# Stores of layer two issued about 25 stages behind their last join, in a macaron block of two routed expert layers around an attention layer

## The chip, the cores and the metric

The kernel runs on one core of a Trainium2 chip. The metric is the device time of one execution in microseconds (us). Three runs of the kernel before took 816.01, 818.97 and 826.0 us; their median is 818.97 us.

## The reference, cut to what matters

The input x has 8 x 512 tokens of 256 values (float32). Three residual layers follow each other, the first and the last with the same weights:

```python
x = x + 0.5 * ffn(layernorm(x), gate_w, w1, w2, w3)     # layer one of experts
x = x + attn(layernorm(x), W_q, W_k, gain, bias, ...)    # top-8 causal neighbours, softmax, gelu
x = x + 0.5 * ffn(layernorm(x), gate_w, w1, w2, w3)     # layer two of experts

def ffn(x, gate_w, w1, w2, w3):                         # 8 experts, 2 of them per token
    probs = softmax(x @ gate_w.T)
    weights, idx = top_k(probs, 2);  weights /= sum(weights)
    out_all = (silu(x @ w1[e].T) * (x @ w3[e].T)) @ w2[e].T      # for each expert e
    return sum over the 2 chosen experts of weights * out_all
```

The change touches only the last step: writing the finished x to the output after layer two.

## The kernel before, in words

The 4096 tokens are 32 token tiles of 128 tokens, and x stays in SBUF (`t_X`) for the whole kernel. An expert layer works like this. The router picks two experts for each token, and GpSimd scatters the split (high and low float16) normalised rows into a list per expert in HBM (`hs`). These lists are cut into 71 expert tiles of 128 rows for each layer, so 142 in all; numbers 0 to 70 belong to layer one, 71 to 141 to layer two. For one expert tile n the work is a pipeline over five engines:

- SyncE (SP in the profile) issues `load` (L1059), a DMA transpose from `hs` to `t_ht`. The ring has four buffers.
- TensorE does `up` (L1227), two groups of 6 matmuls into PSUM; ScalarE does `tanh` (a SiLU, L1360), VectorE `gate` (L1726), ScalarE `high` (L1369) and VectorE `glow` (L1732). The last two write the high and low halves of the gated activation to one of four buffers: three are called `t_gp`, the fourth lies in `t_W`.
- SyncE issues `gt` (L1097), a DMA transpose of these halves to `t_gh` (or, for each fourth tile, within `t_W`). It waits for `glow` of its tile. `high` of tile n waits until the `gt` of tile n-4 has landed, because it overwrites the buffer that was read.
- TensorE does `down` (L1239), 12 matmuls, after the `gt` has landed. ScalarE copies the result out of PSUM (`evict`, L1376), and GpSimd issues `put` (L1000), an indirect DMA that scatters the rows to `yt` in HBM at their token positions.

When all expert tiles that can hold rows of a token tile have been put, SyncE issues `fetch` (L1112): a load of two token tiles (512 KB; the last two are of one tile, 256 KB) from `yt` into `t_hp` or `t_s`. VectorE then does `join` (L1741), two instructions per token tile that add the weighted rows to `t_X`. At the end SyncE issues the ten stores named `out` (L1131 to L1135): seven of four token tiles (512 KB), one of two tiles and two of one tile. Each waits for the joins of its tiles on VectorE and then issues one DMA on SyncE's queue. After the last, SyncE waits for all ten (L1136) and the kernel ends. A transfer by SyncE never waits for VectorE once it is issued; an instruction on SyncE holds up everything behind it on SyncE while it waits or issues.

Nothing on the chip sets the order. Each operation is one letter of a string, `ORDER` (L126 to L155), which is a list of stages: `g` is `out`, `U` is `join`, `J` is `fetch`, `Q` is `gt`, `*` is `put`, `W` is `load`. `Plan.run` (L185 to L205) reads it from left to right. At each letter it takes the waiting operation of this kind with the smallest key, or, with a digit behind the letter, the one at that place of the sorted list. A letter fixes the place of an operation in the sequence of its own engine and no more: a letter of SyncE that is moved leaves the sequences of the other engines as they were. Below, store 0 is the store of token tiles 0 to 3, store 4 that of tiles 4 to 7, and so on.

Of the kernel before, what the change touches and what calls it, by code (L numbers as in the profile page):

```python
# [93 lines left out]
class Want:  # L94
# [55 lines left out]
    "~WWW*s1[hSShPP~~!!*^.N>;V;>^QhQ;WFFu.N;|~h>.EE;!|SS!||**~FF;*~NP.P_~~EQ>;_*F*E~;>~~~EF.*WWQSNNFWQ_S_~;QP.;P>;.S;"  # L150
    ">*N~~S~NPP;.;EEFFWQSPN>;.;EN*uW*uF*W~~E>QSF*~_~;.;NW>;EQQQPSPFS;E>E;.FFWPy1N***SPWEQu;.N>;;S>FQy~WQ.NS_W~Q~*~PP;"
    "E.EQQ;>;;NWWuF_FsSP.N_*>SEP~;;*EFEF*.NSWPyQQQWE>;FF**.;>;~~~.*WNSEEF*~~~P;WuQ>N;S.;NSFPPQQEF**~~>;.;>NSPW;.W;WEE"
    "FNSPQQFEF>;;>***.;.;NNSSWPPJJU>;.;>NUU;SE.;>;;NSWQFPUJJUP>;.NS.UUUWQWJ;>NEFuWPE;JUUUUJJU.FE;>;;>WQNS.UUUN~~~QJFS"
    ";SW;>E**PP.NFJUUUUQJu;;EQWE.SFPP>;;WQJQWE**FF.UNSNP>;;.NSQ*>P*U;*.S;>NSPEEFF**U;U;Q.NSg1gPgPQQ*EEF*FEF*QQE*FJJU*"
    "EEUUFFU*J*g2JgJg1gUUUUggg")  # L155


class Plan:
# [1697 lines left out]
```

## Time and profile before

| | |
|---|---|
| median of three runs | 818.97 us (816.01 to 826.0) |
| the profiled execution's own time | 820.86 us |
| its span, from the first to the last instruction | 819.3 us |
| outside the span | 1.56 us |
| busy: PE, DVE, ACT, POOL | 85%, 69%, 61%, 56% |
| HBM read, written | 33.96 MB, 44.81 MB |
| queue of SyncE (q1): share of the 16 DMA engines' time | 66.8% |
| stores `out`: first and last issue | 788.8 and 816.3 us |

PE is TensorE's matmuls, PEld its weight loads, DVE VectorE, ACT ScalarE, POOL GpSimd, SPq the sequencer of SyncE. The share of the DMA engines is the time that packets are under way on them; in short stretches it passes 1, since packets of one engine overlap. The joins run from 751.1 to 816.2 us, beside the last 14 expert tiles; all that the change moves lies in the last 60 us.

### The profile page before, as it was taken

Reading aid. Unit: us, or ns where it says so; the run is one execution under the profiler, and the core shown is the slowest. Engines: PE = TensorE matmul, PEld = TensorE weight load, DVE = VectorE, ACT = ScalarE, POOL = GpSimd, SP = SyncE. Lnnn points to the kernel's source line nnn. Section 1 sums busy time; section 2 is a strip of 40 time slices with the busy share of each in tenths; the row PEclk is TensorE's granted clock in tenths of the full one; section 3 lists DMA queues with packets and bytes.
Section 4 is the critical chain, followed back from the end, with each engine's and each line's share of the span. In section 5 each row is a group of like instructions: output and inputs, shape, how many; then the busy total and the mean of one; then the engine's idle time right before and its main releaser. Section 6 shows DMA issues by size and latency. Waiting matters only on the chain.

```text
span 819.3 us, 17367 instructions
## 1 busy us (share of the span) xinstructions
PE 694.5 (85%) x4608; PEld 425.3 (52%) x4608; DVE 562.8 (69%) x1596; ACT 498.8 (61%) x972; POOL 456.4 (56%) x545
## 2 busy tenths in 40 slices
PE   1741557999989999999998999999999899999982
PEld 1631224565446665565665555656555456655552
DVE  6779871434577888789889888997766533335953
ACT  4657633444359986877889698976866334343330
POOL 3458888537242645657477654775757854453132
PEclk9965789999999999999999999999999999999997
DMA  8957468888885977889988797899787887779999
GB/s 331 427 198 163 127 175 214 153 158 155 182 155 111 173 150 142 193 162 207 172 172 179 158 197 140 171 180 159 152 164 157 186 173 149 133 146 206 285 247 295
DMA packets 321973, 151.52 MB, mean 185 GB/s; under 512 B 302493, under 2 KB 305949, under 8 KB 321117
## 3 DMA queue, kind: packets, MB, share of 16 engines
q1 hardware_dynamic: 303997, 112.77, 66.8%
q0 software_dynamic: 17888, 37.65, 16.4%
q8 instruction: 46, 0.75, 0.4%
q14 instruction: 42, 0.34, 0.1%
HBM read 33.96 MB, written 44.81 MB: 96 GB/s over the span
## 4 chain that ended last, share of the span: by engine, by line
PE 42%; SPq 13%; DMA 12%; DVE 12%; issue 8%; POOL 6%; ACT 5%; another core or an unknown queue 1%; POOLq 0%; DVEq 0%; ACTq 0%
PE B L1227 22%; PE B L1239 13%; POOL hs L953 4%; SPq L1097 4%; SPq L1059 3%; DMA t_gh<-t_gp 3%; SPq L1044 2%; DMA t_ph<-t_s 2%; PE B L1252 2%; DMA t_ph<-t_p 2%; DMA yt<-t_W,t_idx 1%; PE B L1266 1%; DVE t_th L1726 1%; PE B L1163 1%; DVE t_gp L1732 1%
## 5 line engine op out<-in xcount | busy, mean ns | idle before, releaser
L1227 PE MATMUL B<-t_W,t_ht 128*128 x1704 | 400.2, 383 | 19.6 <-issue 11.3
L1227 PEld LDWEIGHTS B<-t_W,t_ht 128*128 128x128 f16 x1704 | 166.3, 98 | 198.6 <-issue 35.8
L1000 POOL DMA_INDIRECT yt<-t_W,t_idx x107 | 112.2, 1048 | 131.5 <-ACT t_W L1376 97.3
L1726 DVE SCALAR_TENSOR_TENSOR t_th<-B,t_K,t_th 128x512 f32<-128x512 f32 x142 | 105.6, 746 | 108.1 <-PE B L1227 78.6
L1239 PE MATMUL B<-t_W,t_gh 128*128 x1284 | 159.5, 275 | 11.3 <-DMA t_gh<-t_gp 5.7
L953 POOL DMA_INDIRECT hs<-t_s,t_POS x112 | 116.1, 1037 | 65.2 <-issue 28.6
L1239 PEld LDWEIGHTS B<-t_W,t_gh 128*128 128x128 f16 x1284 | 124.4, 99 | 46.7 <-issue 17.3
L1360 ACT ACTIVATE t_th<-B,t_K 128x512 f32<-128x512 f32 x142 | 96.4, 681 | 52.1 <-PE B L1227 34.6
L1732 DVE TENSOR_TENSOR t_gp<-t_th,t_gp 128x512 f16<-128x512 f32 x107 | 75.8, 714 | 34.8 <-ACT t_gp L1369 26.2
L1369 ACT ACTIVATE t_gp<-t_th 128x512 f16<-128x512 f32 x107 | 66.1, 623 | 55.1 <-DVE t_th L1726 36.7
L992 POOL DMA_DIRECT2D t_idx<-hs x142 | 80.3, 570 | 29.3 <-DMA yt<-t_W,t_idx 14.8
L1376 ACT ACTIVATE t_W<-B 128x256 f32<-128x256 f32 x107 | 40.1, 375 | 81.5 <-PE B L1239 50.9
L1000 POOL DMA_INDIRECT yt<-t_yo,t_idx x35 | 36.9, 1054 | 38.5 <-ACT t_yo L1376 28.7
L1324 ACT ACTIVATE t_hp<-t_X,t_ve 128x256 f32<-128x256 f32 x96 | 49.5, 589 | 12.5 <-DVE t_ve L1574 10.5
L942 POOL TENSOR_TENSOR t_ve<-t_ve,t_mhalf 128x4 f32<-128x4 f32 x24 | 27.0, 1125 | 53.6 <-DVE t_ve L1568 52.7
L1239 PE MATMUL B<-t_W 128*128 x420 | 51.8, 273 | 4.4 <-DMA t_W<-t_W 2.6
L1239 PEld LDWEIGHTS B<-t_W 128*128 128x128 f16 x420 | 40.2, 98 | 14.4 <-issue 5.9
L1009 POOL TENSOR_TENSOR t_hp<-t_hp,t_W 128x256 f32<-128x256 f32 x32 | 27.5, 860 | 25.3 <-DVE t_hp L1804 24.9
L1741 DVE SCALAR_TENSOR_TENSOR t_X<-t_hp,t_CW,t_X 128x256 f32<-128x256 f32 x64 | 32.0, 511 | 13.4 <-DMA t_hp<-yt 12.3
L1305 ACT ACTIVATE t_W<-t_W,t_SC 128x1024 f16<-128x1024 f32 x24 | 26.9, 1141 | 19.4 <-DVE t_W L1528 9.1
L1585 DVE TENSOR_TENSOR t_s<-t_hp,t_s 128x256 f16<-128x256 f32 x88 | 36.3, 460 | 1.9 <-ACT t_s L1334 1.9
L1360 ACT ACT_TABLE_LOAD x28 | 35.9, 1283 | 0.5
(206 smaller groups left out, 902.3 us busy)
## 6 DMA issues: line engine op xcount, KB each, us to landing
t_W<-wk SPq DMA_DIRECT2D x6, 2048.0 KB, 15.8
t_hp<-yt SPq DMA_DIRECT2D x16, 512.0 KB
t_s<-yt SPq DMA_DIRECT2D x15, 512.0 KB
t_X<-x SPq DMA_DIRECT2D x8, 512.0 KB, 7.8
out<-t_X SPq DMA_DIRECT2D x7, 512.0 KB
hs<-t_ph SPq DMA_DIRECT2D x22, 136.0 KB
t_ht<-hs SPq DMA_TRANSPOSE x142
t_idx<-hs POOLq DMA_DIRECT2D x142, 0.5 KB
```

The source lines that it names most:

```text
L953: eng.indirect_dma_start(hs_d[L], bass.IndirectOffsetOnAxis(ap=POS[:, k, t + j:t + j + 1], axis=0), SROW[slot][:, 2 * h + j, :], None).the ...
L992: eng.dma_start(IDX[:, n % RING:n % RING + 1].bitcast(F16), hs_d[L][bass.ds(place[n], 128), 512:514]).then_inc(d_id[n % RING], 16)
L1000: eng.indirect_dma_start(yt_d[L], bass.IndirectOffsetOnAxis(ap=IDX[:, n % RING:n % RING + 1], axis=0), YO[n % YR], None).then_inc(d_y[n % ...
L1227: t = eng.matmul(B[b][:], HT[n % HTR][:, (2 * hl + db) * 128:(2 * hl + db) * 128 + 128], W16[:, bass.ds(expert[n] * 4096 + (db * 2048 + wl ...
L1239: t = eng.matmul(B[b][:, 0:256], GH[n % LAG][:, gl, fb * 128:fb * 128 + 128], W16[:, bass.ds(expert[n] * 2048 + (W2OFF + wl * 1024 + fb * ...
L1324: eng.activation(hp[:, j, :], X[:, t0 + j, :], ACT.Identity, bias=ve[:, 2, j:j + 1], scale=ve[:, 1, j:j + 1]).then_inc(s_hp, 1)
L1360: eng.activation(TH[n % THR][:], B[b][:], ACT.Silu, scale=K[:, 0:1]).then_inc(free[b], 1)
L1369: eng.activation(GP[n % LAG][:, 0, :], TH[n % THR][:], ACT.Copy).then_inc(s_gh, 1)
L1376: eng.activation(YO[n % YR], B[b][:, 0:256], ACT.Copy).then_inc(free[b], 1)
L1585: eng.tensor_tensor(s16[:, j, 256:512], hp[:, j, :], s16[:, j, 0:256], ALU.subtract).then_inc(s_lo, 1)
L1726: eng.scalar_tensor_tensor(out=th[:], in0=B[b1][:], scalar=K[:, 7:8], in1=th[:], op0=ALU.mult, op1=ALU.mult).then_inc(free[b1], 1)
L1732: eng.tensor_tensor(gp[:, 1, :], th[:], gp[:, 0, :], ALU.subtract).then_inc(s_gl, 1)
```

## The change

The diff is in `ORDER` only: seven `g` leave their places and stand elsewhere.

```diff
-    "FNSPQQFEF>;;>***.;.;NNSSWPPJJU>;.;>NUU;SE.;>;;NSWQFPUJJUP>;.NS.UUUWQWJ;>NEFuWPE;JUUUUJJU.FE;>;;>WQNS.UUUN~~~QJFS"
-    ";SW;>E**PP.NFJUUUUQJu;;EQWE.SFPP>;;WQJQWE**FF.UNSNP>;;.NSQ*>P*U;*.S;>NSPEEFF**U;U;Q.NSg1gPgPQQ*EEF*FEF*QQE*FJJU*"
-    "EEUUFFU*J*g2JgJg1gUUUUggg")
+    "FNSPQQFEF>;;>***.;.;NNSSWPPJJU>;.;>NUU;SE.;>;;NSWQFPUJJUP>;.NS.UUUWQWJ;>NEFuWPgE;JUUUUJJU.FEg;>;;>WQNS.UUUN~~~QJ"
+    "gFS;SW;>E**PP.NFJUUUgUQJu;;EQWE.SFPP>;;WQJQWE**gFF.UNSNP>;;.NSQ*>P*U;*.S;>NSPEEFF**U;U;Q.NSPPQQ*EEF*FEF*QQE*gFJJ"
+    "U*EEUUFFU*J*JJgUUUUggg")
```

The sequences of TensorE, VectorE, ScalarE and GpSimd stay as they are; only SyncE's is another. Two places matter. The first is the stretch of SyncE's sequence around the fetches of token tiles 10 to 21. `t_ht<-hs` is a `load`, `t_gh<-t_gp` and `t_W<-t_W` are a `gt`, `t_s<-yt` and `t_hp<-yt` are a `fetch`, and `out<-t_X` a store. Before:

```order
L1112 DMA t_s<-yt 128x1024
L1112 DMA t_hp<-yt 128x1024
L1112 DMA t_s<-yt 128x1024
L1059 ISA
L1059 DMA_TRANSPOSE t_ht<-hs 128x4x128
L1097 DMA_TRANSPOSE t_gh<-t_gp 128x8x128
L1097 DMA_TRANSPOSE t_W<-t_W 128x8x128
L1112 DMA t_hp<-yt 128x1024
L1059 ISA
L1059 DMA_TRANSPOSE t_ht<-hs 128x4x128
L1112 DMA t_s<-yt 128x1024
L1097 DMA_TRANSPOSE t_gh<-t_gp 128x8x128
```

And now:

```order
L1135 DMA out<-t_X 128x1024
L1112 DMA t_s<-yt 128x1024
L1112 DMA t_hp<-yt 128x1024
L1112 DMA t_s<-yt 128x1024
L1135 DMA out<-t_X 128x1024
L1059 ISA
L1059 DMA_TRANSPOSE t_ht<-hs 128x4x128
L1097 DMA_TRANSPOSE t_gh<-t_gp 128x8x128
L1097 DMA_TRANSPOSE t_W<-t_W 128x8x128
L1112 DMA t_hp<-yt 128x1024
L1135 DMA out<-t_X 128x1024
```

Stores 0, 4 and 8 are shown in their new places; store 12 follows right behind the second `t_s<-yt`, ahead of the `gt` of expert tile 132. Store 0 now stands ahead of the fetch of tiles 10 and 11, store 4 ahead of the `load` of expert tile 137 and of the `gt` of 130, store 8 ahead of the `load` of 138.

The second place is the end of SyncE's sequence, from the `gt` of expert tiles 136 and 137 on. Before:

```order
L1097 DMA_TRANSPOSE t_gh<-t_gp 128x8x128 x2
L1135 DMA out<-t_X 128x1024 x3
L1097 DMA_TRANSPOSE t_gh<-t_gp 128x8x128
L1097 DMA_TRANSPOSE t_W<-t_W 128x8x128
L1097 DMA_TRANSPOSE t_gh<-t_gp 128x8x128 x2
L1112 DMA t_hp<-yt 128x1024
L1112 DMA t_s<-yt 128x1024
L1112 DMA t_hp<-yt 128x1024
L1135 DMA out<-t_X 128x1024
L1112 DMA t_s<-yt 128x512
L1135 DMA out<-t_X 128x1024
L1112 DMA t_s<-yt 128x512
```

And now:

```order
L1135 DMA out<-t_X 128x1024
L1097 DMA_TRANSPOSE t_gh<-t_gp 128x8x128 x3
L1097 DMA_TRANSPOSE t_W<-t_W 128x8x128
L1097 DMA_TRANSPOSE t_gh<-t_gp 128x8x128 x2
L1135 DMA out<-t_X 128x1024
L1112 DMA t_hp<-yt 128x1024
L1112 DMA t_s<-yt 128x1024
L1112 DMA t_hp<-yt 128x1024
L1112 DMA t_s<-yt 128x512 x2
L1135 DMA out<-t_X 128x1024
```

The three stores (4, 0, 8) between the `gt` of 137 and the `gt` of 138 are gone; store 16 stands ahead of the `gt` of 136, and store 20 ahead of the fetches of tiles 24 and on. Ahead of the last two fetches there were stores 20 and 12, and behind them 24 and 16; now only store 24 is left there, behind both fetches. The last three stores (256, 128 and 128 KB) close the sequence in both.

## Rows read from the trace of the kernel before

**Rows 1.** The page: busy time and share by engine; DMA share in 40 slices.

```profile
PE 694.5 (85%) x4608; PEld 425.3 (52%) x4608; DVE 562.8 (69%) x1596; ACT 498.8 (61%) x972; POOL 456.4 (56%) x545
...
DMA  8957468888885977889988797899787887779999
```

**Rows 2.** Chain that ended last, from 740 us: start us, us, what.

```profile
761.74 5.86 DMA t_hp<-yt
...
769.57 2.76 PE B L1227 x12
...
783.45 0.85 issue
...
791.04 7.54 DMA t_gh<-t_gp
...
798.73 4.30 PE B L1239 x36
...
803.08 2.84 another core or an unknown queue
...
807.09 4.28 DMA yt<-t_W,t_idx
...
811.43 3.79 DMA t_s<-yt
...
815.76 0.48 DVE t_X L1741
```

**Rows 3.** Stretches: busy us of PE, PEld, DVE, ACT, POOL; clock, DMA share, GB/s.

```profile
20.00:30.00 10.00, 4.89 (x59) 4.29 (x60) 7.23 (x36) 7.08 (x14) 1.01 (x1) 1.00 1.01 431
770.00:780.00 10.00, 9.99 (x64) 6.08 (x63) 9.33 (x19) 4.08 (x8) 1.88 (x2) 1.00 1.16 270
814.00:816.00 2.00, 0.00 (x0) 0.00 (x0) 1.02 (x3) 0.00 (x0) 0.00 (x0) 0.50 1.05 422
```

**Rows 4.** SyncE's instructions in order of time: start us, us, what.

```profile
761.18 0.52 SPq L1112 DMA_DIRECT2D t_s<-yt  x1
...
764.26 2.61 SPq L1097 DMA_TRANSPOSE t_gh<-t_gp  x1
...
772.31 1.23 SPq L1097 DMA_TRANSPOSE t_gh<-t_gp  x1
...
788.82 2.02 SPq L1135 DMA_DIRECT2D out<-t_X  x3
791.04 3.67 SPq L1097 DMA_TRANSPOSE t_gh<-t_gp  x1
...
810.82 0.43 SPq L1135 DMA_DIRECT2D out<-t_X  x1
...
811.93 4.81 SPq L1135 DMA_DIRECT2D out<-t_X  x5
```

**Rows 5.** ScalarE's instructions in order of time, with the idle before and its releaser.

```profile
771.70 0.63 ACT L1369 ACTIVATE t_gp<-t_th 128x512 f16<-128x512 f32 x1 [4.25 <-DMA t_gh<-t_gp]
...
777.45 0.63 ACT L1369 ACTIVATE t_gp<-t_th 128x512 f16<-128x512 f32 x1 [1.78 <-DMA t_gh<-t_gp]
```

**Rows 6.** VectorE's joins of token tiles 14 and 15, in order of time.

```profile
770.15 1.92 DVE L1741 SCALAR_TENSOR_TENSOR t_X<-t_s,t_CW,t_X 128x256 f32<-128x256 f32 x4
```

**Rows 7.** The ten stores: issue time on SyncE, ns min/median/max, first and last.

```profile
L1135 SPq DMA_DIRECT2D out<-t_X x10: 433/543/1243, 788.8 to 816.3; - x10
```

**Rows 8.** TensorE's instructions in order of time, with the idle before.

```profile
798.73 1.50 PE L1239 MATMUL B<-t_W,t_gh 128*128 x12 [1.25 <-DMA t_gh<-t_gp]
```

**Rows 9.** SyncE's waits in the last 20 us: us in total, times, longest.

```profile
SPq L1137 <- DMA out<-t_X: 2.3, 1, 2.3
```

**Rows 10.** Columns as in Rows 3; a thinly filled stretch of TensorE and its clock.

```profile
648.00:652.00 4.00, 2.38 (x10) 0.77 (x8) 1.12 (x2) 0.99 (x3) 3.39 (x5) 1.00 0.59 183
...
656.00:660.00 4.00, 2.58 (x9) 1.14 (x10) 1.50 (x2) 1.85 (x4) 3.38 (x5) 0.82 1.03 237
```

**Rows 11.** TensorE: one tile's `up` at the lower clock, in order of time.

```profile
657.42 4.22 PE L1227 MATMUL B<-t_W,t_ht 128*128 x12 [2.27 <-DVE t_th L1726]
```

## The prediction, made before the changed kernel ran

> **What bounds the kernel now.** I read the page first. TensorE is busy for 85% of the span and the DMA engines for most of it, with nines in the last four slices, which is where the stores are [rows 1]. Then I followed the chain that ended last from 740 us on, to see which wait ends last at each point [rows 2]. It goes through a fetch of 5.86 us at 761.74 (token tiles 12 and 13, on which a join waits that stands ahead of a gate), then almost without a break through TensorE to 789 us, through a `gt` transpose of 7.54 us from 791.04 to 798.59, through the last `down` groups on TensorE, a piece of 2.84 us that the profile gives to no queue that it knows (the 36 matmuls before it end at 803.03 and the last 12 follow with 1.4 us, so 1.5 us of it lie behind TensorE's end), the last `put` with 4.28 us, the last fetch with 3.79 us, the last join and the last store. Third, stretches and SyncE's timeline: TensorE is busy for 9.99 of 10 us in 770 to 780 while the DMA engines stand at a share of 1.16 [rows 3]. So in this part two resources are nearly full at the same time, TensorE and the DMA engines, and behind 804 us there is only a chain of transfers.
>
> **What the change removes, adds and moves.** The amount of work is the same: ten stores, the same bytes. Only SyncE's sequence is another. Seven stores of 512 KB move; six of them go to an earlier place in the sequence, and the seventh (24) stays near its place but comes behind the last two fetches. Prices of one such store: on SyncE 0.54 us of issue in the median, 1.24 at most [rows 7]; on the DMA engines its bytes at the best rate that the trace shows over 10 us, 431 GB/s at a share of 1.01 [rows 3]: 524 KB / 431 GB/s = 1.22 us, my estimate.
>
> The Trainium skill ("DMA: Bandwidth & Descriptors", section Specifications) gives about 358 GB/s as the limit of HBM for one core. By it a store would be 1.46 us and the sum below -0.5 instead of -0.75. The trace speaks against that limit here, with 431 GB/s over 10 us of loads.
>
> Step A, **stores 0, 4, 8 and 12 go in between 761 and 773 us.** Do they wait for joins? The last join that one of them needs is that of tile 15; it ends at 770.15 + 1.92 = 772.07 [rows 6], and store 12 stands right ahead of the `gt` that was issued at 772.31 [rows 4]. So waiting costs nothing; what is queued behind them pays for issue and transfer. Store 0 stands ahead of the fetch at 761.18, and so of the one at 761.74 that the chain passes. Stores 0 and 4 stand ahead of the `gt` at 764.26 [rows 4] (expert tile 130), which landed just before 771.70: ScalarE stood idle for 4.25 us until then [rows 5]. It has no slack. All four stand ahead of the `gt` at 772.31 (tile 132), for which ScalarE waited 1.78 us until 777.45 [rows 4, 5]. Both `gt` are read by TensorE right away. Lower end of the price: 0, if the stores fill gaps between the transposes (270 GB/s in 770 to 780 against 431 at best [rows 3]). Less than nothing is excluded, since everything in this stretch stands behind the added stores. Upper end: four transfers of 1.22 and four issues of 0.54, all in a row: 4.9 + 2.2 = 7.1 us. I take **+2.4 us**, two transfers: those that stand ahead of the `gt` with no slack. What comes later is partly covered, as TensorE then has its own queue of `up` groups; the DMA share of 1.16 says that it won't be near zero.
>
> Step B, **stores 4, 0 and 8 leave the place at 788.82.** There they took SyncE 2.02 us. The `gt` behind them (tile 138) was issued at 791.04 and took SyncE 3.67 us [rows 4], landed 7.54 us after its issue [rows 2], and TensorE stood idle for 1.25 us until it had landed [rows 8]. With the stores gone it is issued about 2 us earlier and no longer stands behind 1.5 MB (3.7 us). TensorE is full before it and the other three `gt` are in time, so only the idle time comes back: **-1.25 us**; ends 0 (something else is late then, the `gt` of 139 to 141) and -1.25. Store 16 goes in two `gt` ahead of 788.82, before the `gt` of 136. TensorE reads that after 24 more matmuls of `down` and 12 of `up`, over 5 us of its own work (36 of `down` took 4.30 us, 12 of `up` 2.76 [rows 2]), so 1.22 + 0.54 us are covered; without that cover they would be paid in full, which the range holds.
>
> Step C, **store 20 goes ahead of the fetches at 800.** Their joins are not the last ones, and the chain runs through the `put` meanwhile. I put this at nothing; it is hidden by the chain from 798.73 to 811.4. If that cover fails, it costs its 1.22.
>
> Step D, **the last fetch.** Store 12 was issued at 810.82, ahead of the last fetch at 811.43, which took 3.79 us [rows 2, 4]. Now no store stands directly ahead of it: **-1.2 us** (one transfer), ends 0 and, if its own issue gap goes too, -1.7.
>
> Step E, **the end.** At 811.93 SyncE began to issue five stores in a row [rows 4], and at 814 to 816 the DMA engines ran at 422 GB/s and a share of 1.05 [rows 3]: the last store queued behind others, and SyncE waited 2.3 us for it [rows 9]. Stores 12 and 16 (1 MB, 2.4 us of transfers) now lie far ahead. I take **-0.5 us**; ends 0 and -2.3, which would be the whole wait.
>
> The Trainium skill ("DMA: Bandwidth & Descriptors", section "Anatomy of one DMA") gives about 2.0 us plus the bytes over 436 GB/s for one DMA, a fit that it made on the other descriptor path. For 128 KB that is 2.3 us, the same as the wait that the trace shows, so by it step E would bring nothing and the sum would be -0.25.
>
> Sum: +2.4 - 1.25 + 0 - 1.2 - 0.5 = -0.55 us. The unnamed wait of 1.5 us behind TensorE's end may be a `put` that landed late because of traffic, and may shrink as well; since nothing names it, I take -0.2 of it, with the ends 0 and -1.5. That makes **-0.75 us**. The profiled execution took 820.86 us, 1.56 more than its span and 1.9 more than the median. The sum is of differences, so I add it to the median: 818.97 - 0.75 = **818.2 us**.
>
> **The rivals.**
>
> Rival 1, slower: a full DMA queue. If the DMA engines have no gaps between 761 and 780, all four stores delay all that follows, TensorE's work from 784 on starts later by all of that, and nothing in the last 35 us of matmuls can take it back. For it: the share of 1.16 beside two waits of ScalarE on a landing, and a chain that passes through a fetch of 5.86 us where store 0 goes in. Against it: 270 GB/s is well under 431, and the share counts packets under way, not a limit. Its time: 7.1 - 1.25 - 1.2 - 0.5 = +4.15, so 823.1 us. It decides from the point at which the added delay passes the 3 us that steps B, D and E bring.
>
> Rival 2, slower: the clock. If TensorE is left thin for some microseconds in 765 to 785, its granted clock may fall from 2.4 towards 1.2 GHz. In this trace it did after 648 us: it was busy for 2.38 of 4 us, and the clock stood at 0.82 in 656 to 660 [rows 10]; the 12 matmuls that followed took 4.22 us against 2.76 at full clock [rows 2, 11]. On top of rival 1 that is two or three such groups, +3 to 4.4 us: about 826.5 us. [...]
>
> Rival 3, faster: the stores fill gaps. Step A costs nothing, and the tail gets its upper ends: -1.25, -1.7, -1.5 for the unnamed wait and some 1 us at the end: -5.4, so 813.6 us. For it: the DMA engines move 270 GB/s there, and behind 811 they run at 422, which is a queue that could have been empty. Against it: two `gt` without slack.
>
> Rival 4: the change does not do what it says, as SyncE reaches the new places late and the stores start where they did. The joins end ahead of the new places (step A), so I hold it for unlikely. Its time is that of before, 819.0 us.
>
> **The numbers.** Chances: forecast, within 2 us of 818.2, 0.42; rival 1, 0.22; rival 2, 0.05; rival 3, 0.28; rival 4, 0.03. The predicted time is that of the forecast. The range reaches from rival 3 nearly to rival 2, leaves out rival 2 and what is beyond rival 3, and takes in that the median of three moves by itself, as the runs lie between 816.01 and 826.0: **813 to 824.5 us**. A change under 2% (16.4 us) cannot be told from none in a measurement of this kernel. No case above comes near that, so faster by over 2%: 0.02, within 2%: 0.95, slower by over 2%: 0.03, the rest for what I haven't thought of.
>
> **What the profile after would show.** Step A: ScalarE's wait for the `gt` of 130 and 132 longer than 4.25 and 1.78 us, or not (then rival 3); idle time of TensorE in 764 to 785 of about 2.4 us more, or 5 and more (rival 1); a granted clock under 1.0 there (rival 2). Step B: no idle time of TensorE on the `gt` of 138, and its landing in under 5 us. Step D: the last fetch in about 2.6 us. Step E: less than 2.3 us of wait at the end, and the DMA engines idle at times behind 812. Rival 4: stores issued at 788 or later, more than three in a row. The prediction is wrong if TensorE's last `down` moves by more than 4 us either way, or if another transfer (the last `put`) changes by more than the fetch does.

## The result: slower by 1.1%, and the profile after

The changed kernel took 826.21 us in the median of 17 runs (820.33 to 836.47), the kernel before 818.97 in as many. The ratio is 1.0109 with a 95% interval of 1.0082 to 1.0136, so about 9 us slower. That is clear of no change, though the prediction held that nothing under 2% could be told from none. The forecast was 818.2 us in a range of 813 to 824.5; the time lies outside, on the slow side, where rivals 1 and 2 were.

The profiled execution of the changed kernel is an unusually slow one (836.47 us, span 834.9). Its first 750 us are the same program as before and already 9.2 us later. So I compare the two from one event that lies ahead of all that the change touches: seven tile-halves of `up` in a row, 42 matmuls, which is the last such block before the joins. It starts at 741.62 us in the profile before, at 750.81 after:

```profile
750.81 9.23 PE L1227 MATMUL B<-t_W,t_ht 128*128 x42
```

From this block to the end the kernel before needs 819.3 - 741.62 = 77.7 us and the changed one 834.9 - 750.81 = 84.1 us: 6.4 us more. All times called "from the block" below are counted from it.

TensorE's instructions in order of time after the change (start us, us, what, idle before and its releaser), against [rows 2, 8]:

```profile
780.41 4.31 PE L1227 MATMUL B<-t_W,t_ht 128*128 x12 [3.48 <-DVE t_th L1726]
784.55 1.47 PE L1239 MATMUL B<-t_W,t_gh 128*128 x12
785.87 2.75 PE L1227 MATMUL B<-t_W,t_ht 128*128 x12
788.46 1.47 PE L1239 MATMUL B<-t_W 128*128 x12
793.92 2.74 PE L1239 MATMUL B<-t_W,t_gh 128*128 x12 [4.00 <-DMA t_gh<-t_gp]
796.46 3.14 PE L1227 MATMUL B<-t_W,t_ht 128*128 x12
...
811.85 4.09 PE L1239 MATMUL B<-t_W,t_gh 128*128 x36
...
819.46 1.50 PE L1239 MATMUL B<-t_W,t_gh 128*128 x12 [0.89 <-ACT t_yo L1376]
```

The `up` of expert tile 136 (12 matmuls) waited 3.48 us, the `down` of 132 another 4.00 us for its `gt`; before, the first waited 1.82 us and the second none:

```profile
769.57 2.76 PE L1227 MATMUL B<-t_W,t_ht 128*128 x12 [1.82 <-DVE t_th L1726]
...
777.51 1.50 PE L1239 MATMUL B<-t_W,t_gh 128*128 x12
```

Both groups ran longer, too: 4.31 us for what took 2.76 [rows 2], and 2.74 us for what takes 1.47 two rows above. That is the granted clock: its mean was 0.66 of full speed in 780 to 785 us, between its two levels of 1.2 and 2.4 GHz (the row stands in the last section). The last lines show the other side: `down` of 136, 137 and 138 now follow in one piece of 36 matmuls, where 138 had waited 1.25 us [rows 8].

The first of the two waits comes by way of the fetches. The `up` of 136 waited for a gate, and on VectorE this gate stands behind the joins of token tiles 10 to 12, which waited for their fetches. Before:

```profile
765.20 1.92 DVE L1741 SCALAR_TENSOR_TENSOR t_X<-t_s,t_CW,t_X 128x256 f32<-128x256 f32 x4 [0.40 <-DMA t_s<-yt]
767.62 1.04 DVE L1741 SCALAR_TENSOR_TENSOR t_X<-t_hp,t_CW,t_X 128x256 f32<-128x256 f32 x2 [0.50 <-DMA t_hp<-yt]
768.59 0.74 DVE L1726 SCALAR_TENSOR_TENSOR t_th<-B,t_K,t_th 128x512 f32<-128x512 f32 x1
```

And after:

```profile
771.01 0.68 DVE L1732 TENSOR_TENSOR t_gp<-t_th,t_gp 128x512 f16<-128x512 f32 x1
...
775.56 1.92 DVE L1741 SCALAR_TENSOR_TENSOR t_X<-t_s,t_CW,t_X 128x256 f32<-128x256 f32 x4 [2.04 <-DMA t_s<-yt]
778.50 1.00 DVE L1741 SCALAR_TENSOR_TENSOR t_X<-t_hp,t_CW,t_X 128x256 f32<-128x256 f32 x2 [1.01 <-DMA t_hp<-yt]
779.42 0.74 DVE L1726 SCALAR_TENSOR_TENSOR t_th<-B,t_K,t_th 128x512 f32<-128x512 f32 x1
```

The gate starts 28.6 us from the block instead of 27.0, and the `up` of 136 is as late, +1.6. (The first of these rows is `glow` of tile 132; it matters below.)

ScalarE's two waits for a landing, which answer to [rows 5], have grown from 4.25 and 1.78 us:

```profile
783.95 0.63 ACT L1369 ACTIVATE t_gp<-t_th 128x512 f16<-128x512 f32 x1 [7.31 <-DMA t_gh<-t_gp]
...
793.86 0.63 ACT L1369 ACTIVATE t_gp<-t_th 128x512 f16<-128x512 f32 x1 [5.81 <-DMA t_gh<-t_gp]
```

SyncE's instructions after the change, which answer to [rows 4]:

```profile
769.84 0.45 SPq L1135 DMA_DIRECT2D out<-t_X  x1
770.39 0.38 SPq L1112 DMA_DIRECT2D t_s<-yt  x1
770.81 0.88 SPq L1112 DMA_DIRECT2D t_hp<-yt  x1
771.73 0.49 SPq L1112 DMA_DIRECT2D t_s<-yt  x1
772.38 0.35 SPq L1135 DMA_DIRECT2D out<-t_X  x1
772.86 1.78 SPq L1059 DMA_TRANSPOSE t_ht<-hs  x1
774.73 4.25 SPq L1097 DMA_TRANSPOSE t_gh<-t_gp  x1
779.08 2.59 SPq L1097 DMA_TRANSPOSE t_W<-t_W  x1
781.72 0.57 SPq L1112 DMA_DIRECT2D t_hp<-yt  x1
782.46 0.34 SPq L1135 DMA_DIRECT2D out<-t_X  x1
782.93 1.81 SPq L1059 DMA_TRANSPOSE t_ht<-hs  x1
784.79 0.60 SPq L1112 DMA_DIRECT2D t_s<-yt  x1
785.55 0.35 SPq L1135 DMA_DIRECT2D out<-t_X  x1
786.00 1.98 SPq L1097 DMA_TRANSPOSE t_gh<-t_gp  x1
```

The stores themselves take SyncE 0.34 to 0.45 us. But the transpose behind two of them, the `gt` of 130, now holds SyncE for 4.25 us instead of 2.61, and all behind it is issued later: the `gt` of 132 at 786.00, 35.2 us from the block, against 772.31, 30.7 us, before. Its data were ready long before, since `glow` of 132 ended at 771.69: from 769.84 on, SyncE goes from one issue to the next with hardly a pause, and the `gt` only waits for its place in the sequence. From store 0 to this `gt` SyncE takes 16.2 us, where from the fetch of tiles 10 and 11 to it it had taken 11.1: 2.0 of the added 5.0 are the places of the four stores, 1.6 the longer hold of the `gt` of 130, 1.4 the longer issue of fetches and loads (the stretch begins 0.5 earlier). The `gt` of 132 landed just before ScalarE went on at 793.86, 7.9 us after its issue against 5.1. So the `down` of 132 is 4.5 us late by issue and 2.7 by landing, 7.2 in all.

Last, the stretches of 20 us, counted from the block (columns as in [rows 3]). The kernel before:

```profile
741.62:761.62 20.00, 20.00 (x113) 10.84 (x111) 13.05 (x26) 7.64 (x14) 5.21 (x8) 1.00 1.01 237
761.62:781.62 20.00, 18.17 (x107) 10.10 (x105) 17.81 (x37) 6.52 (x13) 5.69 (x6) 1.00 1.15 266
781.62:801.62 20.00, 17.72 (x122) 11.58 (x121) 9.14 (x16) 7.58 (x16) 4.97 (x7) 1.00 1.13 259
```

The changed kernel:

```profile
750.81:770.81 20.00, 20.00 (x113) 10.87 (x111) 13.48 (x26) 7.75 (x14) 5.28 (x8) 1.00 1.06 242
770.81:790.81 20.00, 15.64 (x83) 8.18 (x80) 14.22 (x30) 5.34 (x10) 3.53 (x4) 0.91 1.06 303
790.81:810.81 20.00, 16.36 (x92) 9.62 (x93) 10.38 (x19) 6.41 (x14) 4.03 (x5) 0.91 0.93 210
```

In the middle 20 us the DMA engines move 303 GB/s instead of 266. That is 0.74 MB more, while the four stores are 2.1 MB: the rest of the traffic gave way to them, and TensorE does 83 matmuls instead of 107. In the next 20 us they move 210 against 259, 1.0 MB less, about what the stores themselves explain: three of 0.52 MB have left this stretch and one, store 16, has come in. The granted clock is at 0.91 in both.

The tail, from the chain that ended last (start us, us, what):

```profile
822.48 5.97 DMA yt<-t_W,t_idx
...
828.52 3.32 DMA t_s<-yt
```

And SyncE's wait for the last store, against [rows 9]:

```profile
SPq L1137 <- DMA out<-t_X: 1.4, 1, 1.4
```

The last fetch takes 3.32 us instead of 3.79, the wait for the last store is 1.4 instead of 2.3. The last `put`, though, takes 5.97 instead of 4.28.

### The profile page after: what moved, and what is told of

It reads as the page before. It is cut to its first block, busy times and chain, and to the rows that moved or that the text cites. A ratio compares the mean times of both kernels' runs of the same rounds, so it can differ in the third digit from the quotient of the medians.

```text
span 834.9 us, 17377 instructions
## 1 busy us (share of the span) xinstructions
PE 702.1 (84%) x4608; PEld 427.5 (51%) x4608; DVE 563.8 (68%) x1596; ACT 498.7 (60%) x972; POOL 455.8 (55%) x545
## 4 chain that ended last, share of the span: by engine, by line
PE 36%; DVE 13%; DMA 12%; SPq 8%; ACT 6%; issue 5%; another core or an unknown queue 2%; POOL 1%; ACTq 0%; DVEq 0%; POOLq 0%
PE B L1227 20%; PE B L1239 13%; DMA t_ph<-t_p 4%; DVE t_th L1726 2%; SPq L1059 2%; DMA t_hp<-yt 2%; SPq L1097 2%; DVE t_gp L1732 2%; SPq L1044 2%; DMA t_gh<-t_gp 1%; DVE t_X L1741 1%; DMA t_ph<-t_s 1%; DMA t_ht<-hs 1%; DVE t_s L1585 1%
## 5 line engine op out<-in xcount | busy, mean ns | idle before, releaser
L1227 PE MATMUL B<-t_W,t_ht 128*128 x1704 | 406.7, 388 | 20.2 <-DVE t_th L1726 8.8
L1000 POOL DMA_INDIRECT yt<-t_W,t_idx x107 | 109.8, 1027 | 136.8 <-ACT t_W L1376 104.4
L953 POOL DMA_INDIRECT hs<-t_s,t_POS x112 | 118.0, 1054 | 65.4 <-issue 28.8
L1000 POOL DMA_INDIRECT yt<-t_yo,t_idx x35 | 36.5, 1044 | 45.6 <-ACT t_yo L1376 30.5
L1239 PE MATMUL B<-t_W 128*128 x420 | 53.8, 280 | 6.3 <-DMA t_W<-t_W 3.5
L1585 DVE TENSOR_TENSOR t_s<-t_hp,t_s 128x256 f16<-128x256 f32 x88 | 38.0, 479 | 1.9 <-ACT t_s L1334 1.9
L1741 DVE SCALAR_TENSOR_TENSOR t_X<-t_s,t_CW,t_X 128x256 f32<-128x256 f32 x64 | 30.3, 488 | 11.5 <-DMA t_s<-yt 10.3
```

Source lines behind the costliest of these rows:

```text
L953: eng.indirect_dma_start(hs_d[L], bass.IndirectOffsetOnAxis(ap=POS[:, k, t + j:t + j + 1], axis=0), SROW[slot][:, 2 * h + j, :], None).the ...
L1000: eng.indirect_dma_start(yt_d[L], bass.IndirectOffsetOnAxis(ap=IDX[:, n % RING:n % RING + 1], axis=0), YO[n % YR], None).then_inc(d_y[n % ...
L1227: t = eng.matmul(B[b][:], HT[n % HTR][:, (2 * hl + db) * 128:(2 * hl + db) * 128 + 128], W16[:, bass.ds(expert[n] * 4096 + (db * 2048 + wl ...
L1239: t = eng.matmul(B[b][:, 0:256], GH[n % LAG][:, gl, fb * 128:fb * 128 + 128], W16[:, bass.ds(expert[n] * 2048 + (W2OFF + wl * 1024 + fb * ...
L1585: eng.tensor_tensor(s16[:, j, 256:512], hp[:, j, :], s16[:, j, 0:256], ALU.subtract).then_inc(s_lo, 1)
L1741: xs.on(eng.scalar_tensor_tensor(out=X[:, tile, :], in0=yg[:, k, :], scalar=CW[:, k, tile:tile + 1], in1=X[:, tile, :], op0=ALU.mult, op1= ...
```

## The experiments

Three theories stood against each other. **Theory 1**: the bytes of the four early stores fill the DMA engines in a stretch that is full already; transposes and a fetch without slack land later, and TensorE starves. **Theory 2**: the loss comes from stores 16, 20 and 24. **Theory 3**: it is SyncE's issue slots and waits for joins. All ratios are against the kernel before on the same chip; its median was 810.4 us in the first four experiments, 808.0 in the next four, 819.1 and 808.5 in the last two sets, so only ratios are compared. In the diffs a line is one operation of SyncE's sequence, by its name and its tile.

**The change in two halves.** First the four early stores alone:

```diff
 load 136
+store 0
 fetch 10, fetch 12, fetch 14
+store 4
 load 137, gt 130, gt 131, fetch 16
+store 8
 load 138, fetch 18
+store 12
 gt 132
...
 gt 137
-store 4, store 0, store 8
 gt 138
...
 fetch 30
-store 12
 fetch 31
```

> The kernel before with stores 0, 4, 8 and 12 at their new early places and stores 16, 20 and 24 where they were. Theory 1 (the transfers of the four early stores fill the DMA engines ahead of transposes and a fetch without slack, and TensorE starves in the 20 us behind them): as slow as the change, 6 to 9 us above the kernel before (ratio 1.008 to 1.011). Theory 2 (the loss comes from stores 16, 20 and 24, of which 16 and 20 stand ahead of the last transposes and fetches): within 2 us of the kernel before (ratio 0.997 to 1.002), as steps A and B of the prediction nearly cancel.

Measured: ratio 1.0093 (1.0059 to 1.0127), that is +7.5 us: as theory 1 says. Then the other half, with 0, 4, 8 and 12 left alone:

```diff
 load 141
+store 16
 gt 136, gt 137, store 4, store 0, store 8, gt 138, gt 139, gt 140, gt 141
+store 20
 fetch 24, fetch 26, fetch 28
-store 20
 fetch 30, store 12, fetch 31, store 24
-store 16
```

> The other half: stores 16, 20 and 24 at their new places, stores 0, 4, 8 and 12 where they were. Theory 1: no loss, 0 to 2 us below the kernel before (ratio 0.997 to 1.000). Theory 2: 5 to 8 us above it (ratio 1.006 to 1.010). In the profile, TensorE's idle time in front of down of tiles 130 to 133 is as before under theory 1.

Measured: ratio 0.9995 (0.9969 to 1.0021). Theory 2 is out; the whole loss sits in the four early stores. The profile of e1_early (814.22 us) has the same two places as the changed kernel. TensorE, in order of time:

```profile
757.83 2.76 PE L1227 MATMUL B<-t_W,t_ht 128*128 x12 [3.34 <-DVE t_th L1726]
760.96 1.50 PE L1239 MATMUL B<-t_W,t_gh 128*128 x12 [0.38 <-DMA t_gh<-t_gp]
...
771.42 2.74 PE L1239 MATMUL B<-t_W,t_gh 128*128 x12 [5.06 <-DMA t_gh<-t_gp]
773.95 3.99 PE L1227 MATMUL B<-t_W,t_ht 128*128 x12
```

With its block at 728.36, the down of 132 starts 43.1 us from it, against 35.9 before (777.51 - 741.62). Behind a wait of 3.34 us the 12 matmuls of `up` still take 2.76; behind the one of 5.06 us the 12 of `down` take 2.74 instead of 1.47 and the next 12 of `up` 3.99 instead of 2.76. So the clock adds 1.27 + 1.23 = 2.5 us here. In the changed kernel it took another 1.55 us of the `up` of 136, ahead of the second wait, and yet the `down` of 132 starts at the same 43.1 us from the block: TensorE waited for the `gt` in any case, so those 1.55 us cost nothing.

The profile of e2_late (814.01 us) is level at the places of the early stores, but TensorE stood idle for 2.70 us instead of 1.25 ahead of the `down` of 138, whose `gt` now has store 16 and the three at 788.82 ahead of it in the sequence. It ended 1.9 us later, and the tail was 1.5 us shorter.

**Bytes or slots.** The changed kernel with tiny early stores:

```diff
-eng.dma_start(out_d[:, t:t + n, :], X[:, t:t + n, :]).then_inc(d_o, 16)
+if t < 16:
+    eng.dma_start(out_d[:, t:t + 1, 0:16], X[:, t:t + 1, 0:16]).then_inc(d_o, 16)
+else:
+    eng.dma_start(out_d[:, t:t + n, :], X[:, t:t + n, :]).then_inc(d_o, 16)
```

> The changed kernel, in which stores 0, 4, 8 and 12 write only 16 columns of their first token tile (8 KB instead of 512 KB, the rest of these 16 token tiles is never stored): same issue slots and waits on SyncE, nearly no bytes. Theory 1 (transfers): the loss is gone and the tail is shorter, 1 to 5 us below the kernel before (ratio 0.994 to 0.999). Theory 3 (it is the issue slots and waits on SyncE that hold up the transposes): still 5 us or more above it (ratio 1.006 or more).

Measured: ratio 0.9984 (0.9950 to 1.0018). With the same sequence, slots and waits, but 32 KB instead of 2 MB, the loss is gone: theory 3 is out. The tail has 2 MB less there, too; the run with the tiny stores in their old places (e9_tiny_before, below) has the same bytes and a ratio of 0.9982, so the early places of the slots cost nothing that can be seen. In the one profile the slots do delay the `gt` of 132: it is issued 2.1 us later from the block and the `down` of 132 comes 2.8 us later, but by TensorE's end 0.2 us of that is left. With `t:t + 2` in place of the 16 columns, half of the bytes:

> The changed kernel in which stores 0, 4, 8 and 12 write only their first two token tiles (256 KB instead of 512 KB each, the other two tiles of each are never stored). Between e4_tiny (0.998) and the change (1.011). If the loss goes with the bytes: ratio 1.003 to 1.006. If it comes as a step once the queue is full (or when the clock falls): near one of the two ends, under 1.001 or over 1.008.

Measured: ratio 1.0075 (1.0042 to 1.0109). Half of the bytes bring more than half of the loss; a straight line from e4_tiny to the change would pass at 1.0047, which is inside the interval, so the form of the curve stays open.

**Which of the stores.** Stores 0 and 4 at their early places, 8 left at 788.82, and the reverse:

> The kernel before with stores 0 and 4 alone at their new early places, ahead of the fetches of tiles 10 to 15 and of the load of 137 and the gt of 130; store 8 stays alone at 788.82, the rest as before. If each early store costs about the same (the transfers add up to one queue): half of e1_early, 3 to 5 us above the kernel before (ratio 1.004 to 1.006). Rival (the price is made at the gt of 132, with stores 8 and 12 right ahead of it): within 1.5 us of the kernel before.

> The other half of e1_early: stores 8 and 12 early, ahead of the load of 138 and of the gt of 132; 0 and 4 at 788.82. If the prices add up: 3 to 5 us above the kernel before (ratio 1.004 to 1.006). Rival (the gt of 132 pays): 6 us or more above it.

Measured: 1.0049 (1.0024 to 1.0073) and 1.0033 (1.0008 to 1.0057), +4.0 and +2.7 us. Their sum, 0.82%, is near the 0.93% of the four, and 8 and 12 alone cost a little less than I had expected. No single transpose pays it all: with stores 8 and 12, TensorE waited 5.23 us for the `gt` of 132; with 0 and 4, it waited ahead of the `up` of 136 instead, and its clock fell there. From the profile of e5_0_4:

```profile
761.88 4.33 PE L1227 MATMUL B<-t_W,t_ht 128*128 x12 [4.05 <-DVE t_th L1726]
```

**Another queue, another order.** e1_early with the four stores issued by ScalarE on its own DMA queue:

```diff
 # SyncE
-elif kind == "out":
+elif kind == "out" and key[0] >= 16:
 # ScalarE
+elif kind == "out" and key[0] < 16:
+    t, n = key
+    for i in range(t, t + n):
+        e.wait_ge(s_x, joined(1, i))
+    eng.dma_start(out_d[:, t:t + n, :], X[:, t:t + n, :]).then_inc(d_o, 16)
```

> e1_early with the four early stores issued by ScalarE on its own DMA queue, at the same stages. If the loss comes from the order in SyncE's queue (transposes stand in line behind the stores' packets, and SyncE is held at issue), the loss shrinks to under half, ratio under 1.005. Rival (the 16 DMA engines are shared and full, whichever queue the bytes are in): as slow as e1_early, ratio 1.008 to 1.011.

Measured: 1.0069 (1.0042 to 1.0095). It lies between the two expectations; its interval overlaps that of e1_early, so no gain from the other queue is shown, and most of the loss stays. In its profile the `gt` of 130 still held SyncE for 4.40 us, with no store in SyncE's queue ahead of it. TensorE waited in another place, 5.26 us ahead of the `up` of 136, whose gate stands behind a join that waited 3.52 us for its fetch, and not at all ahead of the `down` of 132. Nor is the run a clean test of the queue, since ScalarE now waits for the joins itself: it stood idle for 3.87 us ahead of a copy at 762.74, until a join had ended. The Trainium skill ("DMA: Bandwidth & Descriptors", section "Issuing engines are not separate DMA queues") says that transfers from all queues run on the same 16 DMA engines and interleave, whichever engine started them; that hold of 4.40 us and the loss that stays agree with it.

The stores behind the transposes instead of ahead of them:

```diff
 gt 130, gt 131
+store 0, store 4
 fetch 16, load 138, fetch 18, gt 132
+store 8
 fetch 20, gt 133
+store 12
...
 gt 137
-store 4, store 0, store 8
 gt 138
```

(Store 12 leaves its place between the last two fetches, as in e1_early.)

> The four stores in the same 15 us, but each behind the transposes instead of ahead of them: 0 and 4 behind the gt of 131, 8 behind the gt of 132, 12 behind the gt of 133. If it matters what stands right behind a store: the gt of 130 lands as before and the loss is under half of that of e1_early, ratio 1.000 to 1.004. Rival (the stretch is full, 2 MB more in it cost their transfer wherever they stand): ratio 1.006 or more.

Measured: 1.0106 (1.0079 to 1.0132). I had bet on the order, and by the ratio the order brings nothing: 2 MB more in these 15 us cost as much behind the transposes as ahead of them. The one profile does not show it as clearly. It is of an execution of 808.61 us, where the five others took 813.0 to 817.0, and in it the first wait is as before and only the second has grown:

```profile
754.52 2.76 PE L1227 MATMUL B<-t_W,t_ht 128*128 x12 [1.73 <-DVE t_th L1726]
...
766.92 2.16 PE L1239 MATMUL B<-t_W,t_gh 128*128 x12 [4.43 <-DMA t_gh<-t_gp]
```

With its block at 726.47 the `down` of 132 is 4.6 us late, not 7.2, and the end of the span 3.0 us, against 6.7 in the profile of e1_early. Why the other executions take longer than this one no trace shows.

**The same bytes elsewhere.** What did the four stores cost where they stood? The kernel before with them tiny (the diff of e4_tiny):

> The kernel before in which stores 0, 4, 8 and 12 write only 16 columns of their first token tile, in their old places (the rest of these 16 token tiles is never stored): what 2 MB of stores cost where they stood. If a store costs the same wherever it stands (the DMA engines are full to the end): as much is saved as the early places cost, 7 us or more (ratio 0.991 or less). If the old places were nearly free: 1 to 3 us below the kernel before (ratio 0.996 to 0.999).

Measured: 0.9982 (0.9949 to 1.0014), so about 1.5 us for 2 MB, not told apart from nothing, and 4.2 us at most. And extra stores of 512 KB of weights to a scratch tensor, in the kernel before:

```diff
 for kind, key in P.order:
+    if (kind, key) in extra:
+        eng.dma_start(junk_d[extra.index((kind, key))], W[:, 2, :]).then_inc(d_junk, 16)
```

> The kernel before with four extra stores of 512 KB (a constant part of the weights, written to a scratch tensor that nobody reads) ahead of the gt of tiles 116, 118, 120 and 122, at some 700 to 719 us, where the DMA share is 0.77 at 134 to 150 GB/s and no fetch runs. Theory 1 (the price is that of a stretch in which fetches already fill the DMA engines): 0 to 2 us above the kernel before (ratio 1.000 to 1.0025). Rival (any 2 MB of stores put ahead of transposes cost this): 6 us or more (ratio 1.007 or more).

> The same four extra stores ahead of the fetch of tiles 10 and 11, the load of 137, the load of 138 and the gt of 132, which are the places of the early stores; the real stores stay where they were. Theory 1: as e1_early or more, since nothing leaves the tail: 7 to 10 us above the kernel before (ratio 1.009 to 1.012). Rival (it is the waits of the real stores for joins that cost): under 3 us.

Measured: 1.0024 (0.9995 to 1.0053) at 700 to 719 us, 1.0080 (1.0047 to 1.0114) at the early places. The second is a little under the 1.009 that I had expected and inside the interval of e1_early: stores that wait for no join cost there what the real ones cost. Where no fetch runs, 2 MB cost 1.9 us, not told apart from nothing. The difference of the two is 4.5 us; their intervals overlap by 0.0006. The stretch in the profile of e14_junk_early, counted from its block at 728.24:

```profile
748.24:768.24 20.00, 15.38 (x83) 8.14 (x80) 13.93 (x29) 5.35 (x10) 3.71 (x4) 0.91 1.15 299
768.24:788.24 20.00, 16.46 (x89) 9.52 (x90) 10.49 (x20) 6.35 (x13) 3.69 (x4) 0.83 0.91 245
```

The same picture as the change: 299 GB/s and 83 matmuls, and a low clock in both stretches.

**Steps B and D by themselves.** Stores 4, 0 and 8 moved from 788.82 to behind fetch 28, where SyncE waits for a put:

```diff
 gt 136, gt 137
-store 4, store 0, store 8
 gt 138, gt 139, gt 140, gt 141, fetch 24, fetch 26, fetch 28
+store 0, store 4, store 8
 store 20, fetch 30, store 12, fetch 31
```

> The kernel before with the three stores at 788.82 us (4, 0, 8) moved later, behind the fetch of tiles 28 and 29, so no store is in the way of any transpose. Tests step B by itself: 1.25 us less idle time of TensorE ahead of down of tile 138. Step B as predicted: 1 to 2 us below the kernel before (ratio 0.997 to 0.999). Rival (the 1.5 MB now lie ahead of the last put and of the last fetches, where the chain runs through transfers): the end moves out by one to three transfers of 1.22 us less the 1.25, so 0 to 2.5 us above (ratio 1.000 to 1.003).

Measured: 1.0042 (1.0020 to 1.0064), +3.4 us: worse than even the rival. The chain of this kernel, then two of its stretches:

```profile
793.72 6.21 DMA yt<-t_W,t_idx
...
800.00 6.17 DMA t_s<-yt
```

```profile
795.00:800.00 5.00, 0.00 (x0) 0.00 (x0) 4.81 (x11) 0.00 (x0) 0.00 (x0) 0.61 1.02 415
800.00:805.00 5.00, 0.00 (x0) 0.00 (x0) 1.17 (x3) 0.00 (x0) 0.00 (x0) 0.50 1.04 418
```

TensorE did end earlier, 59.9 us from the block against 62.8, and the tail gave back all of it: the last `put` took 6.21 us and the last fetch 6.17, against 4.28 and 3.79 [rows 2], while the DMA engines ran at 415 to 418 GB/s. From the block to the end this profile is level with the one before, 77.7 us in both, so it explains why nothing was gained but not the +3.4 us of the ratio. One store of the three behind the `gt` of 141, and store 12 beside store 20:

```diff
 gt 137, store 4, store 0
-store 8
 gt 138, gt 139, gt 140, gt 141
+store 8
 fetch 24, fetch 26, fetch 28
+store 12
 store 20, fetch 30
-store 12
 fetch 31
```

> The kernel before with store 8 moved from 788.82 to behind the gt of 141, and store 12 beside store 20. Step B for one store of three: the wait of 1.25 us on the gt of 138 nearly gone and 0.5 MB more in the tail: 0.5 to 1.5 us below the kernel before (ratio 0.998 to 0.9995). Rival (each store behind 800 us holds up the last put and fetch by its transfer): even or up to 2 us above.

Measured: 0.9997 (0.9967 to 1.0027): the rival, even. Step D was tested by moving store 12 alone, once to behind the last fetch, once to beside store 20:

> The kernel before with store 12 moved from between the last two fetches to behind them. Tests step D by itself: the last fetch lands 1.2 us earlier. Step D as predicted: 0.5 to 1.5 us below the kernel before (ratio 0.998 to 0.9995). Rival: its bytes now stand ahead of the last store and keep the end where it is, or put it out by 1 us (ratio 1.000 to 1.0015).

> The kernel before with store 12 beside store 20, behind the fetch of tiles 28 and 29, where SyncE then waits 6.8 us for a put. Its bytes flow while SyncE waits: 0.5 to 2 us below the kernel before (ratio 0.9975 to 0.9995). Rival: they hold up the put for which SyncE waits, and the time is the same or up to 1.5 us longer.

Measured: 1.0020 (0.9989 to 1.0050) and 0.9989 (0.9962 to 1.0015). The first moved as it should inside and not at the end. Its last fetch in the chain:

```profile
811.97 2.95 DMA t_s<-yt
```

It took 2.95 us, 0.84 less than before, but the kernel is not faster. Neither run is told apart from the kernel before. No version that I tried beats it.

## Why the prediction was wrong, point by point

**What bounds the kernel.** Right: two nearly full resources in this stretch, TensorE and the DMA engines. I did not draw the conclusion that such a stretch has no room for 2 MB.

**Step A is the step that failed.** It read: "I take **+2.4 us**, two transfers: those that stand ahead of the `gt` with no slack. What comes later is partly covered, as TensorE then has its own queue of `up` groups". The first half holds well enough: the `gt` of 130 landed 33.1 us from the block instead of 30.1 (783.95 - 750.81 and 771.70 - 741.62), +3.1. The second half is wrong. The delay did not get covered, it grew: at the `gt` of 132, for which [rows 5] showed a second wait without slack, it was +7.2, in the changed kernel and in e1_early alike. That is the upper end of my price, 7.1 us for four transfers and four issues in a row, and not two transfers. The cover was missing because SyncE's own sequence was full: the data of the `gt` of 132 were ready 14 us before its issue, so TensorE's queue of `up` groups had no part in when it was issued. A second path that step A named and did not price, the fetch ahead of a join ahead of a gate, made the `up` of 136 late by 1.6 us.

On top came the clock, rival 2: with 1.27 us at the `down` of 132 the next `up`, of 138, started 45.6 us from the block against 37.4, +8.3, and it ran 0.38 us longer itself. The 1.55 us at the `up` of 136 lie ahead of the wait for the `gt` of 132 and are contained in it.

Behind that, what could take the delay back were above all TensorE's own pauses of before, 0.18, 0.85 and 1.25 us, of which step B had counted the last. With the tiny stores, 2.6 of the 2.8 us came back by TensorE's end; of a delay three times as large such pauses can't take back more.

So the mechanism is rivals 1 and 2 together, to which I gave 0.22 and 0.05. What spoke for them were rows that I had: a DMA share of 1.16, and two waits of ScalarE for a landing. I argued against them with 270 GB/s being under 431; but 431 is the rate of plain loads, and in this stretch, with its transposes, the engines stand at a share of 1.15 at 266 GB/s. Taking bytes per second as the measure of room was the error behind the step. e14_junk_early shows it most plainly. That four transfers and four issues add up to nearly the measured 7.2 is in part luck: the slots, the longer holds of transposes and fetches and the later landing share it in other parts than my sum has them.

**Step B** happened as written (TensorE waits no longer for the `gt` of 138, -1.25 us) and was worth less: TensorE then stood 0.89 us ahead of its last `down`, released by ScalarE's copy. It was 8.0 us late at the `down` of 136 and 7.4 at its end. In e3_v1 the step gave more, 2.9 us by TensorE's end; this run and e15_8_later show that in the kernel before such a gain is lost in the tail if the stores go there. That store 16 is covered holds in the changed kernel, but not where the three stores stay (2.70 us in e2_late).

**Step C**, nothing for store 20: no run speaks against it. The changed kernel's last `put`, the piece of the chain that was to hide it, took 5.97 us instead of 4.28, but that of e1_early, where store 20 stays, took 6.03; the spread of one `put` from kernel to kernel (4.28 to 6.21 in the chains above) is larger than the step. e2_late holds 16, 20 and 24 together at 0 within 0.3%.

**Steps D and E** had the right sign in the profile: -0.5 us against -1.2 for the last fetch, and the wait at the end -0.9 against -0.5. The unnamed wait of 1.5 us is gone, and the longer `put` (+1.7) takes its place. The tail from TensorE's end to the end of the span is 13.9 us against 14.9 (834.9 - 820.96, with the last `down` ending at 819.46 + 1.50; before 819.3 - 804.4). So the two profiles differ by 7.4 - 0.95 = 6.4 us from the block on. Both signs that the prediction had named as speaking against it came: TensorE's last `down` moved by more than 4 us, and the last `put` changed by more than the fetch. The rest up to the 9 us of the ratio is not in this pair of executions; e1_early alone gives +7.5 us by its ratio, and its interval (4.8 to 10.3 us) holds both.

**Rival 3**, the gaps: wrong. There were none. **Rival 4** is out: the stores were issued where the sequence says. By the fit that the prediction took from the Trainium skill ("DMA: Bandwidth & Descriptors", section "Anatomy of one DMA"), made on the other descriptor path, the wait for the last store would have stayed at 2.3 us; it shrank to 1.4.

What stays open: how much of the loss the clock makes, since nothing here changes the clock alone; whether the loss is a straight line in the bytes (e11_half); how much the order matters (e8_behind: the ratio says not at all, the one profile says some); and e13_junk_before, whose one profile (819.88 us) shows a wait of 3.5 us and a clock of 0.83 in 711 to 731 us, more than its ratio bears out.

## What to carry to other kernels

A transfer that nobody waits for still has a price, and it is set by its place: the same four stores cost 7 to 9 us among the fetches and transposes and about 1.5 us or nothing where they had stood. Before moving bytes to an earlier place, look for transposes or loads there that are already waited for, and at the share of time in which the DMA engines are busy and not only at their GB/s; the share alone does not decide it either, since it is 1.05 in the tail, where the same bytes cost little. Look, too, at whether the issuing engine has pauses. Where it has none, everything behind an added transfer is issued later, however long its data have been ready; count the full sum of the added transfers and issues then, less only the pauses that the compute engine shows further on, and look at what the clock does after the stall.

## What the runs showed of the hardware that I had not expected

TensorE's granted clock fell behind single waits in an otherwise full stretch. In the changed kernel 5 us around the first wait had a mean of 0.66 of full speed:

```profile
780.00:785.00 5.00, 4.59 (x17) 2.03 (x18) 4.45 (x10) 1.05 (x2) 0.00 (x0) 0.66 1.22 221
```

After waits of 3.48 (this one), 4.05 and 5.06 us the next 12 matmuls took 4.31, 4.33 and 2.74 us, against 2.76, 2.76 and 1.47; after 3.34 us, in e1_early, they took 2.76, as at full clock. It is not the length of the wait alone that tells them apart, for in e14_junk_early a shorter one was followed by a slow group:

```profile
757.22 4.05 PE L1232 MATMUL B<-t_W,t_ht 128*128 x12 [2.87 <-DVE t_th L1731]
```

A transpose holds SyncE at its issue for longer when stores and fetches are under way: the `gt` of 130 for 4.25 us with stores 0 and 4 ahead of it, 2.61 us with the fetches alone [rows 4], and 4.40 us in e7_act, where the stores were issued by ScalarE. So full DMA engines also delay what stands behind a transpose in the sequence.
